# A graph network's second layer by edge counts for 22 of 49 blocks of targets, with the one-hot products that make the counts added to the first layer

## The reference

```python
# layer 0: attention with 4 heads; p = x @ W_proj
e = exp(leaky_relu(src_score[src] + tgt_score[dst], 0.2))
x = layernorm(x + segment_sum(p[src] * e, dst) / segment_sum(e, dst) + bias)
# layer 1, "the second layer" here: a mean over the incoming edges
agg = segment_sum(x[src] @ W_msg.T, dst) / max(deg, 1)
x = layernorm(x + layernorm(relu(x @ W_self.T + b_self + agg)) * gamma + beta)
# layer 2: softmax weights per source; layer 3: a maximum over edges by relation
```

## Time and profile before

| | before |
|---|---|
| median of 3 runs | 4589.87 us (4589.16 to 4594.28) |
| span of the profiled execution | 5974.2 us (the page gives no time around it) |
| PE busy | 2467.8 us, 41% |
| DVE busy | 2086.7 us, 35% |
| ACT busy | 830.0 us, 14% |
| POOL busy | 3220.8 us, 54% |
| mean granted TensorE clock | 0.553 of 2.4 GHz |
| HBM read, written | 403.82 MB, 142.41 MB |

### The profile page before, as it was taken

How to read it: one execution, slowest core, us unless ns; L and a number is a source line. 1 busy time by engine, 2 the same in 40 slices (tenths; PEclk the granted TensorE clock), 3 DMA queues, 4 the chain that set the end, 5 groups by cost and what they waited for, 6 DMA issues and landing times. The chain is left out here.

```text
span 5974.2 us, 63099 instructions
## 1 busy us (share of the span) xinstructions
PE 2467.8 (41%) x16441; PEld 2221.3 (37%) x16441; DVE 2086.7 (35%) x5443; ACT 830.0 (14%) x2496; POOL 3220.8 (54%) x3391
## 2 busy tenths in 40 slices
PE   2344444444333333332766666454566222222221
PEld 1333333333233333331666666344455222222220
DVE  4344434444122222222444344355544122222223
ACT  0111212122000000000322222000001011001112
POOL 3555555554566666664344444545443666666664
PEclk7555555555555555555555555566666556555555
DMA  4222222222122222223333333455555344434443
GB/s 102 57 60 60 61 58 60 59 61 57 41 47 47 47 49 47 48 47 63 115 110 108 107 108 115 130 162 162 162 164 160 93 117 116 108 108 112 112 116 82
DMA packets 427122, 543.15 MB, mean 91 GB/s; under 512 B 116266, under 2 KB 291966, under 8 KB 426862
## 3 DMA queue, kind: packets, MB, share of 16 engines
q1 hardware_dynamic: 311618, 311.80, 17.7%
q0 software_dynamic: 108064, 223.63, 16.6%
q10 hardware_dynamic: 7344, 6.61, 0.4%
HBM read 403.82 MB, written 142.41 MB: 91 GB/s over the span
## 5 line engine op out<-in xcount | busy, mean ns | idle before, releaser
L523 POOL DMA_INDIRECT G<-table,IC x2496 | 2362.6, 947 | 1571.7 <-issue 832.5
L2412 POOL DMA_INDIRECT G<-table,IC x448 | 433.1, 967 | 580.9 <-ACT IC L2271 425.1
L2818 DVE TENSOR_TENSOR_SCAN GW<-BIG,GW,PS 128x512 f32<-128x512 bf16 x208 | 266.2, 1280 | 962.9 <-DMA BIG<-run_mask 620.8
L2412 POOL DMA_INDIRECT G<-table2c,IC x384 | 367.3, 956 | 407.0 <-DMA rows_ahead<-G 148.8
L2780 PE MATMUL PS<-IDENT,GW 128*128 128x128 f32 x840 | 192.5, 405 | 862.3 <-issue 481.4
L1360 PE MATMUL PS<-SEL,G 128*128 128x96 f32 x1664 | 372.1, 417 | 358.1 <-DVE SEL L556 217.1
L1032 PE MATMUL PS<-SEL,GW 128*128 128x96 f32 x1664 | 382.4, 419 | 291.6 <-DVEq L1095 158.9
L1360 PEld LDWEIGHTS PS<-SEL,G 128*128 128x128 f32 x1664 | 359.7, 327 | 365.5 <-DVE SEL L556 220.1
L2780 PEld LDWEIGHTS PS<-IDENT,GW 128*128 128x128 f32 x840 | 158.9, 215 | 887.3 <-issue 495.6
L1032 PEld LDWEIGHTS PS<-SEL,GW 128*128 128x128 f32 x1664 | 356.4, 322 | 304.3 <-DVEq L1095 165.3
L2426 PE MATMUL PS<-BIG 128*128 128x49 f32 x1680 | 387.4, 408 | 60.7 <-issue 31.8
(11 more groups left out here) (314 smaller groups left out, 3749.1 us busy)
## 6 DMA issues: line engine op xcount, KB each, us to landing
rows_ahead<-G SPq DMA_DIRECT2D x104, 520.0 KB
running_max<-BIG SPq DMA_DIRECT2D x105, 512.0 KB
G<-table,IC POOLq DMA_INDIRECT x2944
GW<-source_in_block SPq DMA_DIRECT2D x160, 256.0 KB
ROWSF<-edge_places SPq DMA_DIRECT2D x209, 192.0 KB
BIG<-run_mask SPq DMA_DIRECT2D x104, 256.0 KB
ROWSF<-rows_ahead SPq DMA_DIRECT2D x26, 520.0 KB
SELTF<-rows_ahead SPq DMA_DIRECT2D x26, 520.0 KB
```

Source lines behind the costliest of these rows:

```text
L523: pool.indirect_dma_start(out=G[:, b, u, 0:width], out_offset=None, in_=table, in_offset=bass.IndirectOffsetOnAxis(ap=IC[:, b * U + u:b * ...
L2412: pool.indirect_dma_start(out=GS[:, b, u, 0:width], out_offset=None, in_=table, in_offset=bass.IndirectOffsetOnAxis(ap=IC[:, b * U + u:b * ...
L2818: v.tensor_tensor_scan(RM[:, q, h * 512:(h + 1) * 512], MB[:, q, h * 512:(h + 1) * 512], PS[2 * q + h][:], before, ALU.min, ALU.max).then_ ...
```

## The change

In the first layer's turns 3 to 24 (22 turns, `d` = 0 to 21) the kernel also counts edges. The 16 windows of 8 targets of block `d` (4 windows a group) have up to 256 edges each, two tiles. For each tile DVE makes two bf16 one-hots: `HOTL`, the source's place in its block (128 columns), and `HOTK`, the source's block combined with the target's place in the window (8 x 49 = 392 columns). Their product, two matmuls a window, is the window's count matrix; ACT copies it to `STAGE` in bf16, and SP stores a finished block (1.6 MB) to `COUNTS`. The edge lists by window are gathered in `table0` and unpacked at the start of turn 3.

The second layer becomes a new stage, `edges1_counted`, written out without loops. It gathers only groups 46 to 103 (58 groups). `x` is split into three bf16 parts `XP`; for the first 22 blocks, as 11 chunks, PE multiplies the three parts by the stored counts, loaded in pieces of 7 source blocks (77 pieces with 21 matmuls of 256 columns). The old `edges1` stays behind a flag that also says whether a window has over 256 edges or the first 22 blocks too few; it is skipped where the counts hold. The self term goes through HBM (`SELF`) instead of `HS`. Cut to the core:

```diff
+WN, DB, G0, GL, SPAN, PIECE = 8, 22, 46, 58, 8 * 49, 7    # as constants of their own
 def turn_rows(pe, S, n, nb, kept=False):
     pe.wait_ge(S.rows_ready, n + 2)
+    if kept:
+        pe.wait_ge(S.kept, n + 1)
...
 def keep_self(act, S, n, blk, nb):
     act.wait_ge(S.multiplied, n + 2)
-    a.copy(HS[:, ds(blk, nb), :], rows(PS[7], nb)).then_inc(S.kept, 1)
+    act.wait_ge(S.self_out, n * 16 + 16)
+    a.copy(HSB[:, 0:nb * P], PS[6][:, 0:nb * P]).then_inc(S.kept, 1)
+    act.wait_ge(S.kept, n + 2)
+    act.dma_start(SELF...[:, ds(blk, nb), :], rows(HSB, nb)).then_inc(S.self_out, 16)
...
+def make_hot(dve, d, b, js):
+    keys = dve.snap(d * (2 * WPB) + b * 8, min_val=0, max_val=2 * DWIN - 8)
+    for j in js:
+        q = j % 2
+        dve.wait_ge(counted, window_number(d, b, j) + 1)
+        for tile in range(2):
+            c = 2 * j + tile
+            v.tensor_scalar(HOTK[:, q, tile, :], SPANS, KEYT[:, ds(keys, 8)][:, c:c + 1], None, ALU.is_equal)
+            ins = v.tensor_scalar(HOTL[:, q, tile, :], LOWS, LOWT[:, ds(keys, 8)][:, c:c + 1], None, ALU.is_equal)
+        ins.then_inc(hot_made, 1)
+def count(pe, d, b, js):
+    for j in js:
+        q = j % 2
+        pe.wait_ge(hot_made, window_number(d, b, j) + 1)
+        pe.wait_ge(kept_counts, window_number(d, b, j) + 1)
+        for tile in range(2):
+            last = t.matmul(PS[3 + 4 * q][:, 0:SPAN], HOTL[:, q, tile, :], HOTK[:, q, tile, :],
+                            start=tile == 0, stop=tile == 1)
+        last.then_inc(counted, 1)
+def keep_counts(act, d, s, b, js):
+    for j in js:
+        q = j % 2
+        act.wait_ge(counted, window_number(d, b, j) + 3)
+        if b == 0 and j == 0:
+            act.wait_ge(counts_out, d * 16 + 16)
+        a.copy(STAGE[:, s, :, at:at + WN], PS[3 + 4 * q][:, 0:SPAN]...).then_inc(kept_counts, 1)
...
-def act_group(act, pss, turn, b):
+def act_group(act, pss, turn, b, d=None, s=0):
+    if d is not None and b > 0:
+        keep_counts(act, d, s, b - 1, range(4))
     act.wait_ge(z_ready, i + 2)
     a.activation(WEP[:, q], ZL[:, q], ACT.Exp, bias=NSHIFT0[:]).then_inc(w_ready, 1)
...
+def act_turn(act, pss, turn, d, s):
+    copy_sums(act, S, n, blk, 2, True)
+    act_group(act, pss, turn, 0, d, s)
+    root(act, S, n + 1, 2)
+    act_group(act, pss, turn, 1, d, s)
+    write_rows(act, S, n, blk, 2, X, True)
+    store_rows1(act, S, blk, 2)
+    act_group(act, pss, turn, 2, d, s)
+    copy_turned(act, S, n, 2)
+    act_group(act, pss, turn, 3, d, s)
+    keep_self(act, S, n, blk, 2)
+    if d is not None:
+        keep_counts(act, d, s, 3, range(4))
...
 def pe_group(pe, pss, turn, b, d=None):
-    pe.wait_ge(z_ready, i + 1)
-    node_terms(1 - q, H).then_inc(terms, 1)
+    pe.wait_ge(z_ready, i + 2)
+    node_terms(1 - q, H, 2).then_inc(terms, 1)
...
     last.then_inc(pe_done, 1)
+    if d is not None:
+        count(pe, d, b, range(4))
...
 def dve_group(dve, regs, pss, turn, b, d=None):
...
     dve.sem_inc(parts, 1)
+    if d is not None:
+        make_hot(dve, d, b, range(4))
     w = window(dve, regs[1 - q])
     dve.wait_ge(pe_done, i + 2)
     add_window(dve, w, 1 - q, acc_chain, i + 1, den_chain)
...
+# edges1_counted, PE; ready blocks begin at step l and end at l + 1; pieces lie on steps 4 to 51
+for l in range(END):
+    one, two = step(l)
+    if one:
+        messages(pe, S, one[0], 2)
+    if l < GL:
+        pe.wait_ge(gathered[b], l // RING * (16 * U) + 16 * U)
+        pe.wait_ge(sel_ready, l + 1)
+        pe.wait_ge(added, l + 1)
+        for u in range(U):
+            last = t.matmul(PS[q][:, 0:W], G[:, b, u, 0:D], SEL[:, q, u, :], start=u == 0, stop=u == U - 1)
+        last.then_inc(pe_done, 1)
+    if two:
+        turn_rows(pe, S, two[0], 2)
+    for m in piece_of.get(l, ()):
+        multiply_piece(pe, m)      # 7 blocks x 3 parts, 256 columns each, from PIECES_IN[m % 4]
+    if two:
+        scores(pe, S, two[0], 2)
+# DVE: select and add a group, split x in steps 0 to 3, then mix_messages and scales, keep_scores
```

More of the change, by code:

```diff
@@ L50 @@
 HALF = 4 * P
+WN = 8
+WPB = P // WN
+DB = 22
+DWIN = DB * WPB
+LB3 = -(-(DWIN + 1) // P)
+LW = LB3 * P
+G0 = 46
+GL = GROUPS - G0
+SPAN = WN * NB
+PIECE = 7
+PIECES = NB // PIECE
 class Chain:
@@ L582, in shift_windows, with load_turn @@
             pass_wait(ch.eng)
-        def load_turn(sp, reg, pss, turn, table, n, placed_rows, terms, row_in, win_in):
-            for b in range(RING):
+        def load_turn(sp, reg, pss, turn, table, n, placed_rows, terms, row_in, win_in, slots=range(RING)):
+            for b in slots:
                 at = sp.snap(turn * RING + (b + 1), min_val=1, max_val=GROUPS)
@@ L783, in self_term @@
             for j in range(nb):
[L784 removed]
+                last = t.matmul(PS[6][:, j * P:(j + 1) * P], NST[:, j * P:(j + 1) * P], NW[:, D:2 * D],
                                 start=True, stop=True)
@@ new lines, in turn_keys @@
+            def turn_keys(pe):
+                pe.wait_ge(keys_ready, 1)
+                for lst, bank, rest in ((KEY, 5, 0), (LOWF, 7, 2 * P)):
+                    for i in range(LB3):
+                        for tile in range(2):
+                            to = PS[bank][:, (i * 2 + tile) * P:(i * 2 + tile + 1) * P] if i < 2 else \
+                                PS[6][:, rest + tile * P:rest + (tile + 1) * P]
+                            last = t.transpose(to, lst[:, i, tile * P:(tile + 1) * P], IDENT[:])
+                last.then_inc(keys_turned, 1)
@@ L1387, in _ @@
+                    with pe.If(not_counted(pe)):
+                        t.matmul(PS[1][:, 0:W], ZERO[:, 0:P], ZERO[:, 0:W], start=True, stop=True).then_inc(pe_done, 2)
+                        start_pe(pe, S)
+                        pe.wait_ge(w_in, 96)
+                        with pe.Fori(0, passes(pe)) as pss:
+                            pe.wait_ge(opened, pss + 1)
+                            pe.sem_inc(passed, 1)
+                            with pe.Fori(0, FIRST) as turn:
                                 for b in range(RING):
@@ L1390, in dve_group @@
+                            with pe.If(out_of_order(pe, 4)):
+                                with pe.Fori(FIRST, LAPS) as turn:
+                                    for b in range(RING):
+                                        pe_group(pe, pss, turn, b)
+                    pe.nop()
                 def dve_group(dve, regs, pss, turn, b):
@@ new lines, in _ @@
+                            with dve.If(out_of_order(dve, 4)):
+                                with dve.Fori(FIRST, LAPS) as turn:
+                                    for b in range(RING):
+                                        dve_group(dve, regs, pss, turn, b)
+                            dve.wait_ge(acc_chain, pss * GROUPS + (GROUPS + 1))
+                            pass_wait(dve)
+                        w = window(dve, regs[1])
+                        dve.wait_ge(pe_done, np_ * GROUPS + 2)
```

637 lines of the change are left out of this document (488 added, 149 removed).

## The result

The changed kernel takes 4667.01 us (median of 3 runs, 4666.77 to 4671.17), the kernel before 4589.87: a ratio of 1.0164 with a 95% interval of 1.0148 to 1.0180. It is 77 us slower where 95 us less were forecast: above the forecast's own range of 4400 to 4590, and 2 us above the 4330 to 4665 over all cases. A repetition gave 4669.8 against 4590.5 (1.0178, 1.0161 to 1.0195).

The account below looks back on a forecast made before the run. Gathers sent by POOL were taken to bound the kernel before. 4590 - 440 (second layer) + 324 (first layer) + 20 (rest) = 4494, say 4495 us; forecast's own range 4400 to 4590, over all cases 4330 to 4665.

Parts of the forecast that it names:

- The kernel before is bound by its gathers: Four edge stages: 832 back-to-back gathers each at 1.25 us, a floor of 1040 us; four floors plus 402 give 4562.
- Second layer, the failed step: Inside the layers, the self term's way through memory is loaded a step ahead and costs nothing; second layer 440 us less.
- Waits in a pair of steps: Second layer, a block's two steps: PE waits 1.3 us for VectorE's selection, 5.5 for its statistics; 18 to 27 us a pair.
- PE's prices and clock: Second layer's pieces: a 256-column matmul takes 0.213 us at 1.2 GHz, half at 2.4; high level assumed, 20 us loss.
- The rival of a PE bound at 1.2 GHz: Second layer: dense pieces at 1.2 GHz make a pair of steps 27 us, 163 more, 4658; chance 20%.
- The clock rises in the first layer: First layer: PE at 2.4 GHz makes turns 48.5 us instead of 55, 143 less, 4350; chance 20%.
- First layer, durations and walk: First layer: one-hots 0.79 us a window, third window waits for first count; groups 17.7, 14.0, 12.4, 12.4, taken as 55 a turn.
- A gather and a bf16 operation meet: Where POOL's gather overlaps VectorE's bf16 operation, VectorE pays some 0.24 us for a meeting and POOL nothing.
- First layer, the second step that failed: First layer's loop: 22 turns at 55 us, 1210, within a stage of 1392 us, +324.
- The rest: Between stages: nine gathers, stores, flag steps, a load, one empty stage with barrier; bounds 5 and 45, taken 20 us.
- The changed kernel's span near 6000: In the disturbed profiled execution: 528 us more against 537 less, so a span near 6000 and no gain.
- All of it hidden: First layer: all new work hidden, chain under 40 us a turn, only unpacking and the rest left; 4186, chance 5%.

Follow-up runs that it names:

- the kernel with the later store: Changed kernel with the 1.6 MB store of a turn's counts issued one group later: 4631.82 us, against 4669.8 for the changed kernel beside it.
- l1_order: The new order: changed kernel, first layer's loop written out, two of each group's four windows made within the next group: 4309.33 us.

## Why the prediction was wrong, step by step

- *The kernel before is bound by its gathers*: right for three stages (1043, 1047 and 1044 us against 1040), though read from a disturbed profile. Its check, 4 x 1040 + 402 = 4562 beside the median of 4590, came near by luck: the third stage takes 1135 and the rest of the span 318. The first layer's 28 us of drain were 3; that is 25 of the 45 us missed there.
- *Second layer, the failed step*: "The self term's way through memory inside the layers is loaded a step ahead: nothing." It went by where the load stands in the loop, and that its buffer is free a step ahead, and not by what is in front of it in SP's queue: the store of the block before, which waits for VectorE's scores. With it the stage gives back 337 us instead of 440, and moving it alone gives 123 us. The forecast of 600 us for the stage was right for the work (588 and 587 with the load moved).
- *Waits in a pair of steps*: PE's wait for VectorE's statistics was taken as 5.5 us; its waits of that kind reach 8.6 us with the load in its place and at most 5.6 with the load moved. Its wait for the selection behind the scores was taken as 1.3 and is 2.4. VectorE's own wait for the scores, up to 13 us, stood in no term and costs nothing once the load is out of the way.
- *PE's prices and clock*: 0.213 and 0.107 us a matmul, right; both levels within one run of pieces. The rival of a PE bound at 1.2 GHz gave 4658 and is false all the same. A time that fits isn't a mechanism.
- *The clock rises in the first layer* (4350): it didn't in the part that counts. The sixteen matmuls of a group take 426 ns each on average before and after, and the layer's granted clock is 0.61 against 0.54.
- *First layer, durations and walk*: one-hots 0.79 us a window and the third waiting for the first count: right, each of the four groups 0.2 to 1.0 us shorter than walked. A turn is 53.8 where 55 was taken.
- *A gather and a bf16 operation meet*, "VectorE pays some 0.24 us for a meeting and POOL nothing": read from one meeting, and wrong for POOL, as said above. In the changed kernel it moves nothing, since POOL waits there; in the kernel with the new order it goes with the 24 us that are left.
- *First layer, the second step that failed*: the term "22 x 55 = 1210" walks each turn and has nothing for the return of a longer loop. 8.4 us at each of 10 returns, 84 us, which the smaller turns and a shorter end partly covered. The change doubled the body (two turns) and lengthened the turn, and neither was priced.
- *The rest*: +46 for +20. The start (+10.6) is as worked out; the joint behind the first layer grew by 25.5, and 18 of it is the first layer's chain, which ends 22.7 us behind the last gather.
- *The changed kernel's span near 6000*: it stood at 4665, since it was profiled on an undisturbed chip. On the other it was not measured. But the kernel with the later store, 38 us from it elsewhere, took 5770 us there against 5981, so "no gain" on that chip is likely wrong too.
- *All of it hidden, "the order of the waits does not" allow it*: true of this order, and l1_order shows that another order does.

## What to carry to other kernels

For a transfer that is "ahead", look at what its queue does in front of it: a load stands behind every store ahead of it, with the waits of that store. When a wait is large, ask whether anything late comes of it; the wait of 214 us was worth nothing and the one of 99 us everything, and only taking each away by itself told them apart. Before a loop's body is doubled, look in the profile for instruction packets inside the loop; if they come back at each return, write it out, and keep large stores away from the return.

## What the runs showed of the hardware

- The first layer's loop has no repeated instruction transfers with a body of one turn (56 packets in the whole kernel), and has them with two (110). With counts in the body most returns cost VectorE 8 to 8.7 us, with one turn and with two; 11 more returns cost 111 us. The length at which it starts was not measured.
- A 1.6 MB store issued beside a return lengthens the stall by some 3.5 us (4.21 + 3.86 with it, 3.51 + 1.01 without).
- A gather that overlaps a bf16 one-hot of VectorE is sometimes longer: 23 of 127 over 1.0 us instead of 0.94 in the kernel before, none of the 560 others. Where VectorE is busy for 740 of 860 us, the gathers' pace is 1.284 us instead of 1.252.
- One chip ran the kernel before in 5981 us and the others in 4587 to 4596 (medians). The first profile, with stretches of one matmul per 1.40 us, is as long as the runs on that chip. The instruction packets are no more in it than in the second profile (56 in both); the cause stays open.
